# Copies of a scattered sum added up in DRAM by accumulating transfers, and two chunk loops that run further ahead

## The reference, cut to what matters

```python
h = relu(layernorm(x))
agg = zeros_like(x).at[src].add(edge_attr)          # 100000 rows of 256 added into 6250 rows
x = x + mlp(concat[h, agg, attention(h, u)])        # W1, relu, W2
h = relu(layernorm(x)); ht = relu(h @ W1 + b1)
msg = sigmoid(exp(w) * ht[src] + b)
fsum = segment_sum(msg, dst, 6250)                  # 100000 rows of 256 again
c = (log(s / (1 - s)) - b) / exp(w)                 # s = clip(fsum, 1e-6, 0.9999999)
y = concat[ht, c] @ Wn + bn
out = x + relu(y / norm(y))
```

## Time and profile before

| what | value |
|---|---|
| median of 3 runs | 3076.63 us |
| the profiled execution, its own time | 3074.35 us |
| its span | 3072.6 us |
| busy share of the span: PE, DVE, ACT, POOL | 67%, 72%, 44%, 62% |
| scatters into the four copies | 78 to 460 us of the span |
| gathers and jobs of the first layer | 468 to 1374 us |
| middle | 1374 to 1600 us |
| gathers and jobs of the second layer | 1728 to 2840 us |
| end | 2840 to 3044 us |

### The profile page before, as it was taken

One profiled execution on the slowest core, in us unless ns is written; L12 is line 12 of the kernel. 1 busy time (PEld: TensorE's weight loads), 2 busy tenths in 40 slices (PEclk: granted clock), 3 DMA queues, 4 the chain that ended last, 5 costly groups with the idle time before them and its releaser, 6 DMA issues.

```text
span 3072.6 us, 43572 instructions
## 1 busy us (share of the span) xinstructions
PE 2062.7 (67%) x9239; PEld 1396.6 (45%) x9239; DVE 2204.8 (72%) x6063; ACT 1351.5 (44%) x4324; POOL 1896.5 (62%) x1687
## 2 busy tenths in 40 slices
PE   1469874667777677676667567776776776867653
PEld 1357752554444443444445445434344444444542
DVE  2665546877998998983454588789899799634555
ACT  0133343446556455451125444554554654845234
POOL 0587668777777777734442577777777777773000
PEclk9578876889999999997878768899999999968887
DMA  9898762333333332326656433333333333332222
GB/s 353 235 182 168 153 99 77 98 98 91 102 97 88 100 98 86 102 73 210 199 176 212 152 97 96 95 93 102 89 96 102 86 98 97 106 106 62 86 68 91
DMA packets 192906, 370.57 MB, mean 121 GB/s; under 512 B 32825, under 2 KB 114003, under 8 KB 190114
## 3 DMA queue, kind: packets, MB, share of 16 engines
q0 software_dynamic: 90864, 206.28, 26.4%
q1 hardware_dynamic: 70210, 107.02, 10.6%
q10 hardware_dynamic: 31600, 54.66, 5.0%
HBM read 281.48 MB, written 86.35 MB: 120 GB/s over the span
## 4 chain that ended last, share of the span: by engine, by line
PE 31%; DVE 30%; issue 16%; DMA 8%; POOL 7%; ACT 3%; DVEq 2%; another core or an unknown queue 1%; ACTq 1%; SPq 0%; POOLq 0%
PE bank L1332 28%; DVE agg L1095 11%; POOL store L619 6%; DVE oh L1046 4%; DVE store L1042 4%; DMA store<-g_table,idx_all 3%; DVE hits L1040 3%; DMA agg_copy<-agg 2%; DVE cum L999 2%; DVEq L1095 1%; DMA store<-in_edge_attr,idx_all 1%; DVE store L1036 1%; ACT dist L746 1%; POOL agg_copy L597 1%
## 5 line engine op out<-in xcount | busy, mean ns | idle before, releaser
L1332 PE MATMUL bank<-store,oh 125*128 125x157 f16 (+2 forms) x6770 | 1488.6, 362 | 616.2 <-DVE oh L1046 198.4
L1332 PEld LDWEIGHTS bank<-store,oh 128*128 128x128 f32 (+1 forms) x6770 | 945.4, 164 | 1141.4 <-issue 770.6
L1095 DVE TENSOR_TENSOR agg<-bank,agg 128x256 f32 x1845 | 772.1, 418 | 307.9 <-PE bank L1332 199.3
L619 POOL DMA_INDIRECT store<-g_table,idx_all x785 | 814.1, 1037 | 270.8 <-issue 144.2
L754 ACT ACTIVATE oh<-dist 128x128 f32<-128x128 f32 x1845 | 538.1, 305 | 921.5 <-PE bank L1332 890.1
L619 POOL DMA_INDIRECT store<-in_edge_attr,idx_all x628 | 662.5, 1055 | 208.6 <-issue 121.5
L746 ACT ACTIVATE dist<-iota,nloc_all 128x128 f32<-128x128 f32 x1845 | 582.7, 386 | 62.0 <-DVE idx_all L854 61.1
L597 POOL DMA_INDIRECT agg_copy<-agg x160 | 259.9, 1624 | 190.1 <-ACT agg L712 105.0
L1046 DVE TENSOR_TENSOR oh<-hits,v 125x512 f16<-125x512 f16 x720 | 272.9, 413 | 0.0
L1036 DVE TENSOR_TENSOR store<-iota,ttab 125x628 f16<-125x628 f16 x360 | 170.9, 475 | 92.3 <-PE bank L1332 91.0
L1042 DVE TENSOR_TENSOR store<-iota,jtab 125x820 f16<-125x820 f16 x360 | 207.0, 575 | 0.0
(11 more groups left out here) (196 smaller groups left out, 1596.9 us busy)
## 6 DMA issues: line engine op xcount, KB each, us to landing
agg_copy<-store ACTq DMA_DIRECT2D x4, 6400.0 KB, 29.5
agg<-in_edge_attr SPq DMA_DIRECT2D x39, 512.0 KB, 4.7
store<-in_x SPq DMA_DIRECT2D x72, 256.0 KB, 4.7
msk<-agg_copy ACTq DMA_DIRECT2D x52, 256.0 KB, 4.2
store<-g_table,idx_all POOLq DMA_INDIRECT x785
cum<-agg_copy ACTq DMA_DIRECT2D x48, 256.0 KB, 4.4
store<-in_edge_attr,idx_all POOLq DMA_INDIRECT x628
pre_scratch<-store SPq DMA_DIRECT2D x25, 256.0 KB, 4.7
```

The source lines that it names most:

```text
L619: gp.indirect_dma_start(out=store[:, at % RING * D:(at % RING + 1) * D], out_offset=None, in_=table_dram, in_offset=bass.IndirectOffsetOnA ...
L1095: dve.tensor_tensor(to, pt[n % TB][:, 0:D], to, ALU.add).then_inc(s_acc, 1)
L1332: return pe.matmul(o, l, r, start=start, stop=stop, skip_group_check=skip)
```

## The change

The four copies are no longer added by GpSimd in SBUF. GpSimd issues 24 accumulating transfers from DRAM to DRAM instead, each for an eighth of a copy (128 rows of 1600 numbers, 819200 bytes). They stand between the gathers of the first two groups of the first layer, one behind each eighth gather: in group 0 copy 1 is added into copy 0 and copy 3 into copy 2 in turns (16 pieces), in group 1 copy 2 into copy 0 (8 pieces). The middle loads copy 0 only, with four slots of one buffer, and VectorE adds four chunks ahead of its loop where it added two. In the end TensorE's transposes run three chunks ahead of the product where they ran one, with five PSUM banks for them in place of two.

```diff
+FSLOTS = 4
+PIECES = 8
+PIECE = AROWS // P * D // PIECES
...
+        sums_at = (pA, pB, pS, pR, bank[2])
...
+            def fold_piece(to, by, n):
+                into, off = (aggc_dram[r].rearrange("(p c) f -> p (c f)", p=P)[:, n * PIECE:(n + 1) * PIECE] for r in (to, by))
+                gp.dma_start(into, off, accum_op=ALU.add).then_inc(s_fa, 16)
+
             def gathers(table_dram, g):
...
                                           ).then_inc(s_g[beat_of(g, t) % SLOTS], 16)
+                    n = t // 8
+                    if t % 8 == 7 and g == 0 and n < 2 * PIECES:
+                        fold_piece(*((0, 1), (2, 3))[n % 2], n // 2)
+                    elif t % 8 == 7 and g == 1 and n < PIECES:
+                        if n == 0:
+                            gp.wait_ge(s_fa, 16 * 2 * PIECES)
+                        fold_piece(0, 2, n)
...
-            for n in range(NW):
-                c0, c1, c2, c3 = fold[n % 2]
-                gp.wait_ge(s_fc[n % 2], 16 * COPIES * (n // 2 + 1))
-                gp.tensor_tensor(c0, c0, c1, ALU.add).then_inc(s_fa, 1)
-                gp.tensor_tensor(c2, c2, c3, ALU.add).then_inc(s_fa, 1)
-                gp.wait_ge(s_fa, 3 * n + 2)
-                gp.tensor_tensor(c0, c0, c2, ALU.add).then_inc(s_fa, 1)
...
             def fold_load(n):
-                if n >= 2:
-                    act.wait_ge(s_fi, n - 1)
-                for r in range(COPIES):
-                    act.dma_start(fold[n % 2][r].rearrange("p (j f) -> p j f", j=2), copies[r][n]).then_inc(s_fc[n % 2], 16)
+                if n >= FSLOTS:
+                    act.wait_ge(s_fi, n - FSLOTS + 1)
+                act.dma_start(fold[n % FSLOTS].rearrange("p (j f) -> p j f", j=2), folded[n]).then_inc(s_fc[n % FSLOTS], 16)
...
             act.wait_ge(s_rank, G1 + 1)
-            fold_load(0)
-            fold_load(1)
+            act.wait_ge(s_fa, 16 * 3 * PIECES)
+            for n in range(FSLOTS):
+                fold_load(n)
             for n in range(NW + 2):
                 if n < NW:
                     fold_out(n)
-                if n + 2 < NW:
-                    fold_load(n + 2)
+                if n >= 2 and n - 2 + FSLOTS < NW:
+                    fold_load(n - 2 + FSLOTS)
...
             def fold_in(n):
-                dve.wait_ge(s_fa, 3 * n + 3)
+                dve.wait_ge(s_fc[n % FSLOTS], loads_before(n % FSLOTS) + 16 * (n // FSLOTS + 1))
                 at = agg[:, n * CH:(n + 1) * CH]
-                dve.tensor_tensor(at, fold[n % 2][0], at, ALU.add).then_inc(s_fi, 1)
+                dve.tensor_tensor(at, fold[n % FSLOTS], at, ALU.add).then_inc(s_fi, 1)
...
-            fold_in(0)
-            fold_in(1)
+            for n in range(4):
+                fold_in(n)
             add_sums(0)
             for n in range(NW):
-                if n + 2 < NW:
-                    fold_in(n + 2)
+                if n + 4 < NW:
+                    fold_in(n + 4)
                 if n + 1 < NW:
                     add_sums(n + 1)
...
-                    r = ts(t, (pA, pB)[b][:, :], 1e-6, 0.9999999, ALU.max, ALU.min)
+                    r = ts(t, sums_at[q][:, :], 1e-6, 0.9999999, ALU.max, ALU.min)
...
             def sums_transpose(n):
-                if n >= 2:
-                    pe.wait_ge(s_v4, n - 1 + (n % CHB == 0))
+                if n >= CHB:
+                    pe.wait_ge(s_v4, n - CHB + 1)
...
-            sums_transpose(0)
+            for n in range(CHB - 2):
+                sums_transpose(n)
             for n in range(NW):
-                if n + 1 < NW:
-                    sums_transpose(n + 1)
+                if n + CHB - 2 < NW:
+                    sums_transpose(n + CHB - 2)
                 bundle_product(n)
```

More of the change, by code:

```diff
@@ L273, in gnn_program @@
         raw_src, src_rows = area(EBLK).bitcast(I32), area(EBLK)
-        fold = [[t[:, 2 * CH * c:2 * CH * (c + 1)].bitcast(F32) for c in range(COPIES)] for t in (msk, cum)]
+        fold = [t[:, 2 * CH * c:2 * CH * (c + 1)].bitcast(F32) for t in (msk, cum) for c in range(FSLOTS // 2)]
         w1aT, w1cT, woT = slot2k(oh, 0), slot2k(oh, 1), slot2k(oh, 2)
@@ L310, in gnn_program @@
         s_sa = [sem(f"s_scatter{r}") for r in range(COPIES)]
-        s_fc = [sem(f"s_copies{q}") for q in range(2)]
+        s_fc = s_el
         s_fa, s_ft, s_fe = sem("s_foldadd"), sem("s_foldtr"), sem("s_foldout")
@@ L405, in nth_on_copy, with loads_before @@
             return sum(copy_of(i) == copy_of(t) for i in range(t))
+        def loads_before(q):
+            return 16 * len(range(q, EBLKS, ESLOTS))
         def rows_of(b):
@@ L764, in _ @@
             stage_onehots(0, JOBS1 // QUAD)
-            copies = [t.rearrange("(c j p) f -> c p j f", p=P, j=2) for t in aggc_dram]
+            folded = aggc_dram[0].rearrange("(c j p) f -> c p j f", p=P, j=2)
             def fold_load(n):
-                if n >= 2:
-                    act.wait_ge(s_fi, n - 1)
-                for r in range(COPIES):
-                    act.dma_start(fold[n % 2][r].rearrange("p (j f) -> p j f", j=2), copies[r][n]).then_inc(s_fc[n % 2], 16)
+                if n >= FSLOTS:
+                    act.wait_ge(s_fi, n - FSLOTS + 1)
+                act.dma_start(fold[n % FSLOTS].rearrange("p (j f) -> p j f", j=2), folded[n]).then_inc(s_fc[n % FSLOTS], 16)
             def fold_out(n):
@@ L1625, in sums_transpose @@
             def sums_transpose(n):
-                if n >= 2:
-                    pe.wait_ge(s_v4, n - 1 + (n % CHB == 0))
+                if n >= CHB:
+                    pe.wait_ge(s_v4, n - CHB + 1)
                 for j in range(2):
                     for k in range(KD):
-                        r = pe.transpose((pA, pB)[n % CHB % 2][:, k * WIN + j * P:k * WIN + (j + 1) * P],
+                        r = pe.transpose(sums_at[n % CHB][:, k * WIN + j * P:k * WIN + (j + 1) * P],
                                          agg[:, n * CH + j * D + k * P:n * CH + j * D + (k + 1) * P], ident[:, :])
```

## The result

The changed kernel takes 2969.97 us (median of 4 runs, 2963.22 to 2975.18) where the kernel before took 3071.47 in the same comparison: a ratio of 0.967, interval 0.963 to 0.971. The forecast was 3009 us with a range down to 2980, so the sign and the places were right and the gain was 101 us where 67 were forecast. The profiled execution took 2974.91 us, its span is 2973.0.

The account below looks back on a forecast made before the run. Limits were GpSimd in the first gathers, a VectorE-TensorE loop in the middle, VectorE with waits for transposes in the end. 25 - 16 - 52 - 24 = -67 us on 3074.35 gave 3007, stated as 3009; range 2980 to 3052.

Parts of the forecast that it names:

- The step that failed: Middle's loop: TensorE waits for no fold and becomes the limit, 24 rounds of 5.85 us, -52 us.
- The bound of 5.4 for a higher clock: Middle's loop: at TensorE's higher clock a round could be 5.4 us; the term's bounds were -63 to -25 us.
- The start of the middle: First load to x of chunk 0: fold at 1379 us, x at about 1391, -16 us.
- One sign of being wrong: Middle: the forecast is wrong if VectorE still waits for the loads there.
- The pieces in group 0: Group 0: sixteen pieces at 1.55 us of GpSimd each, gap included, nothing hiding them, +25 us (+13 to +31).
- The transfer: Queue q0 in group 0: a piece takes 6.7 us of all 16 engines, +0 us, +10 if first beats stall.
- rival 3: Queue q0: pieces hold it, queue slower than GpSimd from 8.6 us, gain gone at 12.8; slower than before, chance 0.1.
- The estimate by the Trainium skill: Pieces in group 0: 2.0 us plus bytes at 436 GB/s, 3.9 us a piece; the sum does not move.
- Group 1: Group 1: eight pieces cost 12.4 us or nine gathers of GpSimd's lead, +0 us; +5 if it is used up.
- The end: End: transposes ready before they are asked for, 4.9 us per body, five bodies, -24 us (-12 to -30).

Follow-up runs that it names:

- filler: Kernel before with four idle products ahead of each chunk's transposes in the middle; 3371.33 us beside 3373.71 on another chip, ratio 0.9996.
- heads_deep: Changed kernel with its pieces in the first 48 gathers of groups 1 to 3, eight slots, loads six chunks ahead; 3230.93 us on another chip, ratio 0.957.
- after_again: The changed kernel run once more, unaltered, on one chip with the moved pieces; 2967.02 us, ratio 0.966 to the kernel before.
- half_pieces: Changed kernel with 24 pieces of half the bytes but as many rows; 2969.05 us, ratio 0.966 to the kernel before.
- two_ahead: Changed kernel with two slots and the fold two chunks ahead, still one copy and no GpSimd adds; 3028.13 us, ratio 0.985 to the kernel before.
- heads_again: Changed kernel with the 24 pieces moved to the first 48 gathers of groups 1 to 3; 2945.16 us, ratio 0.959 to the kernel before.
- relu_first: Kernel before with ScalarE's relu put ahead of the four load issues in the middle; 3046.50 us beside 3071.10, ratio 0.994.
- relu_first_filler: Kernel before with both the relu ahead of the loads and the idle products in the middle; 3047.16 us, ratio 0.991.
- best: heads_deep with ten idle products at each turn of the end's loop body; 3224.93 us on the same other chip, ratio 0.956 to the kernel before.

## Why the prediction was right in its places and wrong in the size

**The step that failed** is the one on the middle's loop: "TensorE waits for none and becomes the limit. It is busy 147.9/25 = 5.9 us per chunk; 1.12 + 4.71 = 5.83 by the chain", and its bound, "at TensorE's higher clock a round could be 5.4". The mechanism was right: TensorE's waits on the fold went from 71.5 us over the middle to 2.8. The size of the term was not, since both prices were taken at the granted clock that went with the waiting. Without the waits the clock is 1.00 and a chunk costs TensorE 3.9 us; the round of 4.28 is that and 0.4 us of waits. The term of -52 us measured -89.9, and the 38 us between them are more than the whole miss of 33 us in the span; the start of the middle and the groups went 4 and 3 us the other way.

The 38 us have three parts. From 5.85 to 5.40 us a round, 11 us in all, has nothing to do with the waits that went: 5.40 is what TensorE is busy in the loop of the kernel before, while 147.9 holds the stretch ahead of the first x too (18 us, with the last jobs of the groups), which the sum prices by itself, and the chain's round was one with slow matmuls. From 5.40 to 3.88, 37 us in all, is the change of the matmuls' speed. The waits that are left, 0.4 us a round, take 10 us back. The filler run shows the clock's part by itself: with TensorE kept busy by idle products and the loads and adds as before, the real matmuls went from 5.4 to an estimated 4.1 us a round. The bound of 5.4 for a higher clock was therefore no bound at all, but what the loop took at 0.82.

The right price stood in the trace of the kernel before, in a round at the end of its middle:

```profile
1590.03 0.66 PE L1547 MATMUL bank<-ident,agg 128*128 128x128 f32 x4 [2.24 <-DVE agg L1185]
1590.53 1.89 PE L1332 MATMUL bank<-agg,w1bT 128*128 128x256 f32 x8
1592.26 1.89 PE L1332 MATMUL bank<-w2T,store 128*128 128x256 f32 x8
```

From 1590.03 to 1594.15 that is 4.1 us for a chunk, and 24 rounds of it are 99 us, where 140 were forecast and 102.7 measured.

One sign of being wrong that the prediction named did come: VectorE still waits for loads in the middle, 23.4 us in 16 waits. The loads are no slower (3.4 us to landing, 5.6 at most); the round that has to hide them is shorter. By `heads_deep` this costs 0.4 us a round.

The runs also order what the loop was made of, per round: 8.0 us before; 7.2 with the relu ahead of the loads; 6.5 with one copy, no adds and the fold two ahead; 4.3 with the fold four ahead; 3.8 with eight slots. Depth was worth more than the removed adds and loads, 2.2 against 1.6 us, in this order of steps; no run has four copies with the fold four ahead.

**The pieces in group 0** were right in their mechanism and 4 us too dear: +25 us forecast, and +20.9 in the profiled execution, +17.1 in that of `after_again`. The issue on GpSimd was priced at 1.25 us and is 1.01. That the groups together gave 27.7 us, so near the 25, is luck, since group 1 made up the difference. The transfer was forecast to cost nothing, with 6.7 us of all 16 engines. It took an estimated 4.5 us of them, below the 8.6 from which rival 3 would begin, and the half pieces show that its length does not matter. The slower rival is thereby out. The estimate by the Trainium skill that was weighed there (DMA: Bandwidth & Descriptors, "Anatomy of one DMA") gave 3.9 us; the trace has 7.0 us from issue to landing. The sum did not depend on it.

**Group 1** was forecast at nothing, and +5 us if GpSimd's lead was used up. By the same rows it cost 6.9 us in the profiled execution, and 2.2, 0.0 and 2.8 us in those of `after_again`, `two_ahead` and `half_pieces`. No run has its eight pieces alone. `heads_again` puts 24 pieces in such stretches for 5 us.

**The start of the middle** gave 12 us of 16. The loads waited for nothing, but the fold of chunk 0 began at 1409.9, ten microseconds after the first load as before, because the last 14 jobs of the group were still being added; I had let the load alone decide it. From that fold to x of chunk 0 it took 11.7 us, as forecast.

**The end** came out as followed, 24 us, and 22 us alone.

## What to carry to other kernels

Price a stage that is to be freed of waits by the fastest row of each instruction in the trace, not by its mean: the mean holds the slow clock that went with the waits. And count the busy time over the loop alone, not over the loop with what stands ahead of it. Before removing a limit, ask each engine's queue in turn what stands next; here TensorE made faster alone gave nothing, and the chain then ran through four load issues of ScalarE in front of a relu. And put transfers that one engine must issue where that engine runs ahead of the others, not where a fixed count of steps happens to put them.

## What the runs showed of the hardware

- An accumulating transfer from DRAM to DRAM of 128 rows of 6.4 KB takes GpSimd 1.01 us to issue, as long for half the row, lands after 7.0 us, and takes an estimated 4.5 us of all 16 DMA engines (2.5 for half the row).
- TensorE's granted clock over the loop of the middle, by run, as a mean over its two levels; the idle time is the round less TensorE's busy time:

| run | round, us | idle in a round, us | granted clock |
|---|---|---|---|
| before | 8.0 | 2.6 | 0.82 |
| relu_first | 7.2 | 2.6 | 0.90 |
| two_ahead | 6.5 | 2.1 | 0.93 |
| relu_first_filler | 6.9 | 0.9 | 0.96 |
| filler | 7.8 | 1.8 | 0.99 |
| after | 4.3 | 0.4 | 1.00 |
| heads_deep | 3.8 | under 0.1 | 1.00 |

- So less idle time in a round goes with a faster clock on the whole, but it does not order the runs by itself. In the end of the changed kernel 16 matmuls took 6.5 us behind an idle time of 7.7 us, and in `best` 6.7 us behind one of 3.4 us with idle products ahead of it, while 3.62 us is what they take in the next chunk. Behind idle times of 2.7 us elsewhere in the end of the kernel before the same 16 took 3.69 us in 12 of 15 cases, and 5.1 to 6.7 us in the other three. Why the shorter idle time did not help in `best` is open.
- The same kernel took 3374 us on one chip and 3071 on others. The stretch of gathers and jobs of the first layer took 1035 us there (in the trace of `filler`, where it is the same code) in place of 905, at nearly the same busy time of VectorE (796 and 793 us), and a granted clock of 0.84 in place of 0.91. Why is open.
